# A relu layernorm times an 8192x8192 matrix on one core: x of the later row blocks loaded by GpSimd, behind its power, and not by SyncE

## The chip, the cores and the metric
One core of a Trainium2 chip runs the kernel; the chip's other cores do nothing. The metric is the device time of one execution in microseconds. The median of three runs before the change is 709.2 us (709.12 to 709.41). TensorE is called PE in the profile, VectorE DVE, ScalarE ACT, GpSimd POOL, SyncE SP; a q behind an engine's name means its sequencer, where transfers are issued.

## What is computed
```python
def _layernorm(x, axis=-1, eps=1e-05):
    m = jnp.mean(x, axis=axis, keepdims=True)
    v = jnp.var(x, axis=axis, keepdims=True)
    return (x - m) / jnp.sqrt(v + eps)

def reference(x, adj, L0_gnn_h):          # x, L0_gnn_h: 8192 x 128; adj: 8192 x 8192, all fp32
    h = jnp.maximum(_layernorm(x, axis=-1), 0.0)
    return x + 0.9 * (adj @ h) + 0.1 * L0_gnn_h
```
adj is the bulk: 256 MB of fp32, read once.

## The kernel before, in words
**Product.** The output is computed transposed, 128 features on the partitions, in 16 chunks (columns) of 512 rows of adj, with h as the stationary and adj (transposed on the host) as the moving operand. The contraction runs over 64 blocks of 128 rows of h. For precision both operands are split into a high part that TensorE takes at its fast rate (`fp32r`) and a low remainder: adj into `a_hi` (ScalarE, a copy, L305) and `a_lo` (VectorE, the subtraction, L349), h into `h_hi` (L282) and `h_lo` (L341). Each product is three matmuls: h_hi x a_hi, h_lo x a_hi, h_hi x a_lo (in the wide stage L451, L457, L462; in the tall stage L473, L474, L478). Only block 0 of h and the first six columns of adj for it are taken unsplit (L420).

**Pieces.** adj is read in 256 pieces of 128 x 2048 values, 1 MB each. The wide stage (pieces 0 to 127) does 8 chunks at once in the 8 banks of PSUM: two pieces per block of h, so block k is needed first at piece 2k. The tall stage (pieces 128 to 255) does one chunk after another with four blocks of h to a piece; by then all of h is there. A piece goes to one of 6 slots of `raw`, then to one of 3 slots of `a_hi` and `a_lo`. ScalarE and VectorE take the pieces in order; up to piece 39 VectorE makes `a_lo` in halves of 1024 columns (`LOW_PARTS`), up to piece 9 in quarters (`FINE_LOW`), then in one instruction. TensorE waits for each part of `a_lo` of a piece (`pe.wait_ge(lo_ready, ...)`) ahead of its L462.

**h.** The blocks of h are made in units: unit 0 is blocks 0 to 3, every later unit u = 1 to 30 two blocks, a = 2u + 2 and a + 1, needed by TensorE from piece due = 2a = 4u + 4 on. `GROUPS` is the same with block 0 by itself, so that group g = u + 1 is unit u. For a unit, VectorE takes statistics of x (`bn_stats`, L315, after waiting for `x_landed[u + 1]` in `wait_x`), aggregates them (L325) and adds epsilon (`var_eps`, L328); GpSimd takes the power -0.5 (`rstd`, L268); VectorE makes `shift` (L334); ScalarE makes h (`h_full`, L275) and h_hi; VectorE makes h_lo. x lies in a ring of 24 blocks.

**Order.** The order of each engine's work is written out by piece: tables say behind which piece's own work a step of h is done. For units with a < 20 (u = 1 to 8) the statistics come behind piece due - 6, the aggregate and the power behind due - 4, the shift behind due - 3; for the later ones the statistics come behind due - 6 and due - 5, the aggregate behind due - 5, the shift behind due - 4. h_full comes behind due - 2 and h_hi, h_lo behind due - 1.

**Queues.** SP issues nearly all transfers: for q = 0 to 255 `load_piece(q)`, which waits until the slot is free (from piece 8 on, until VectorE has made `a_lo` of piece q - 6), then at some q a load of residual data or a store. Ahead of `load_piece(q)` it issues the x of a unit where `LOAD_X_AT` says so (L217, in `load_x`): at q = due - 5 for a < 20, at due - 6 after. ScalarE issues x of blocks 1 to 3 and two halves of the first pieces at the start. GpSimd issues none; its loop is the 32 powers (L265 to L269).

Of the kernel before, what the change touches and what calls it, by code (L numbers as in the profile page):

```python
# [44 lines left out]
UNITS = [(0, FIRST)] + [(_b, _b + UNIT) for _b in range(FIRST, BLOCKS, UNIT)]  # L45
GROUPS = [(0, 1), (1, FIRST)] + UNITS[1:]
X_RING, H_RING = 24, 16
# [2 lines left out]

LATE = 20
LOAD_X_AT = {}
STATS_AT, AGGREGATE_AT, SHIFT_AT = {}, {}, {}
SCALE_AT, HIGH_H_AT = {}, {}
for _u in range(1, len(UNITS)):
    _a = UNITS[_u][0]
    _due = QUADS * _a
    if _a < LATE:  # L60
        LOAD_X_AT[_due - 5] = _u
        STATS_AT[_due - 6] = [_a, _a + 1]
        AGGREGATE_AT[_due - 4] = SHIFT_AT[_due - 3] = _u + 1
    else:
        LOAD_X_AT[_due - 6] = _u
        STATS_AT[_due - 6], STATS_AT[_due - 5] = [_a], [_a + 1]
        AGGREGATE_AT[_due - 5] = SHIFT_AT[_due - 4] = _u + 1
    SCALE_AT[_due - 2] = HIGH_H_AT[_due - 1] = _u
# [20 lines left out]
def parts(q):  # L89
    n = PARTS.get(q, 1)  # L90
    width = PIECE // n
    return [(i, slice(i * width, (i + 1) * width)) for i in range(n)]
# [19 lines left out]
def steps_through(q, halves, seg=QUAD - 1):  # L112

    own = next(i for i, end in enumerate(ends(q, halves)) if seg < end) + 1
    return sum(len(ends(k, halves)) for k in range(MIXED, q)) + own
# [6 lines left out]
def unit_of(k):  # L122
    return 0 if k < FIRST else 1 + (k - FIRST) // UNIT
# [9 lines left out]
def build(nc, x, adj_early, adj_wide, adj_tall, res, out):  # L133
# [4 lines left out]
    with ctx:  # L138
        def sb(name, shape, dt=fp32):
            return ctx.enter_context(nc.sbuf_tensor(name, shape, dt))  # L140

        def sem(name):
            return ctx.enter_context(nc.semaphore(name))
# [6 lines left out]
        x_sb = sb("x_sb", [P, X_RING, F])  # L150
# [13 lines left out]
        x_landed = [sem(f"x_landed{n}") for n in range(len(UNITS) + 1)]  # L164
# [13 lines left out]
        h_full_ready = sem("h_full_ready")  # L178
# [18 lines left out]
        def load_part(engine, q, i, cols):  # L197
            n = PARTS[q]
            at = (i % (n // 2)) * (PIECE // n)
            engine.dma_start(raw[:, q % RAW_SLOTS, cols],  # L200
                             adj_early[q, i // (n // 2), :, at:at + PIECE // n]
                             ).then_inc(part_landed[q % RAW_SLOTS][i], 16)

        def in_x(k):
            return k % X_RING
# [5 lines left out]

        @block.sync
        def _(sp):
            def load_x(n, a, b):
                if a >= X_RING:
                    sp.wait_ge(h_full_ready, unit_of(b - 1 - X_RING) + 1)
                sp.dma_start(x_sb[:, in_x(a):in_x(a) + b - a, :], x[:, a:b, :]).then_inc(x_landed[n], 16)  # L217

            def load_piece(q):
                if q >= RAW_SLOTS + NATIVE:  # L220
                    sp.wait_ge(lo_ready, steps_through(q - RAW_SLOTS, LOW_PARTS))
                elif q >= RAW_SLOTS:
                    sp.wait_ge(piece_used, q - RAW_SLOTS + 1)
                if q in PARTS:
                    for i, cols in parts(q):
                        if (q, i) not in BY_SCALAR:
                            load_part(sp, q, i, cols)
                else:
                    source = adj_wide[q - EARLY, :, :] if q < WIDE_PIECES else adj_tall[q - WIDE_PIECES, :, :]
                    sp.dma_start(raw[:, q % RAW_SLOTS, :], source).then_inc(raw_landed[q % RAW_SLOTS], 16)  # L230

            def load_residual(n):
                if n:
                    sp.wait_ge(residual_ready, n)
                sp.dma_start(res_sb[:, :, :], res[FINISH[n][0], :, :, :]).then_inc(res_landed, 16)

            def store(n):
                sp.wait_ge(finished_ready, n + 1)
                sp.dma_start(out[FINISH[n][0], :, :], finished[:, n % 2, :]).then_inc(stored[n % 2], 16)

            load_x(0, 0, 1)
            for q in range(PIECES):
                if q in LOAD_X_AT:
                    u = LOAD_X_AT[q]
                    load_x(u + 1, *UNITS[u])
                load_piece(q)
                if q in RES_LOAD_AT:
                    load_residual(RES_LOAD_AT[q])
                if q - RAW_SLOTS - 1 in FINISH_AT:
                    store(FINISH_AT[q - RAW_SLOTS - 1])  # L250
            last = len(FINISH) - 1
            sp.wait_ge(finished_ready, last + 1)
            sp.dma_start(out[FINISH[last][0], :, 0:SEG // 2],
                         finished[:, last % 2, 0:SEG // 2]).then_inc(stored[last % 2], 16)
            sp.wait_ge(finished_ready, last + 2)
            sp.dma_start(out[FINISH[last][0], :, SEG // 2:SEG],
                         finished[:, last % 2, SEG // 2:SEG]).then_inc(stored[last % 2], 16)
            sp.wait_ge(stored[(last + 1) % 2], 16 * ((last + 1) // 2))
            sp.wait_ge(stored[last % 2], 16 * (last // 2 + 2))

        @block.gpsimd
        def _(pool):
            nc.gpsimd.memset(warm[:, :], 0.0).then_inc(warm_ready, 1)
            nc.gpsimd.memset(exponent[:, :], -0.5).then_inc(exponent_ready, 1)
            pool.wait_ge(exponent_ready, 1)  # L265
            for g, (a, b) in enumerate(GROUPS):
                pool.wait_ge(var_eps_ready, g + 1)
                nc.gpsimd.tensor_tensor(rstd[:, a:b], var_eps[:, a:b], exponent[:, 0:b - a],  # L268
                                        ALU.pow).then_inc(rstd_ready, 1)  # L269

        @block.scalar
        def _(act):
# [40 lines left out]
        def _(dve):  # L313
# [30 lines left out]
            def low_a(q):  # L344
                for _, cols in steps(q, LOW_PARTS):
                    dve.wait_ge(hi_ready, steps_through(q, PARTS, cols.stop // SEG - 1))
                    if cols.start == 0 and q >= MIXED + SPLIT_SLOTS:
                        dve.wait_ge(piece_used, q - SPLIT_SLOTS + 1)
                    nc.vector.tensor_tensor(a_lo[:, q % SPLIT_SLOTS, cols], raw[:, q % RAW_SLOTS, cols],  # L349
                                            a_hi[:, q % SPLIT_SLOTS, cols].bitcast(fp32),  # L350
                                            ALU.subtract).then_inc(lo_ready, 1)
# [37 lines left out]
            for q in range(MIXED, PIECES):  # L389
                low_a(q)  # L390
                for k in STATS_AT.get(q, []):
                    wait_x(k)
                    last = statistics(k)
                    if any(k == end - 1 for _, end in GROUPS):
                        last.then_inc(stats_ready, 1)
                if q in AGGREGATE_AT:
                    aggregate(AGGREGATE_AT[q])
                if q in SHIFT_AT:
                    make_shift(SHIFT_AT[q])
                if q in HIGH_H_AT:  # L400
                    low_h(HIGH_H_AT[q])
                if q in FINISH_AT:
                    finish(FINISH_AT[q], slice(0, SEG))
                if q in RES_SUM_AT:
                    add_residual(RES_SUM_AT[q])
# [108 lines left out]
```

## Time and profile before

| | before |
|---|---|
| median of 3 runs | 709.2 us (709.12 to 709.41) |
| the profiled execution's own time | 709.23 us |
| its span in the profile | 707.4 us |
| PE, DVE, ACT, POOL busy | 702.4, 636.1, 531.6, 31.5 us |
| moved by the DMA engines | 285.75 MB, 404 GB/s in the mean |

The span runs from the first to the last recorded instruction; 1.8 us of the execution's time lie around it. Times of the rows below count from the start of the span. A row of the timeline gives start, duration, engine, line and operation, output<-inputs, how many instructions are merged in it, and in brackets how long the engine was idle before and what ended that.

### The profile page before, as it was taken

What the parts mean: (1) busy time and instruction counts of PE and PEld (TensorE: products, weight loads), DVE (VectorE), ACT (ScalarE), POOL (GpSimd) and SP (SyncE); (2) the same over time, 40 slices, a digit from 0 to 9 for tenths busy, and PEclk for the clock granted to TensorE, in tenths of its full rate; (3) what the DMA queues carried; (4) which work ended last, traced back from release to release, by engine and by line L of the source; (5) the groups of instructions that cost most, each with busy time, mean ns of one, the idle gap of its engine ahead of it and who ended that gap; (6) DMA issues with size and microseconds to landing.
All of it is one profiled execution on the core that took longest, in us unless ns stands there. A gap on an engine that the chain in (4) does not pass through costs nothing.

```text
span 707.4 us, 8192 instructions
## 1 busy us (share of the span) xinstructions
PE 702.4 (99%) x3088; PEld 578.4 (82%) x3088; DVE 636.1 (90%) x567; ACT 531.6 (75%) x465; POOL 31.5 (4%) x38
## 2 busy tenths in 40 slices
PE   8999999999999999999999999999999999999998
PEld 5888888888888888888888888888888888888886
DVE  5999999999989999999998888888988898889885
ACT  5899988788788788778776767676767676767673
POOL 1101110000000000000000000000000000000000
PEclk9999999999999999999999999999999999999999
DMA  9999999999999999999999999999999999999990
GB/s 365 417 418 420 416 419 416 419 416 418 420 416 419 417 419 417 419 416 420 421 418 418 388 409 389 404 401 399 414 421 414 424 420 423 422 419 422 406 414 21
DMA packets 46551, 285.75 MB, mean 404 GB/s; under 512 B 5168, under 2 KB 9520, under 8 KB 14000
## 3 DMA queue, kind: packets, MB, share of 16 engines
q1 hardware_dynamic: 46080, 283.99, 98.0%
q10 hardware_dynamic: 432, 1.25, 0.5%
q8 instruction: 24, 0.39, 0.2%
q14 instruction: 15, 0.12, 0.0%
HBM read 281.02 MB, written 4.19 MB: 403 GB/s over the span
## 4 chain that ended last, share of the span: by engine, by line
PE 99%; DMA 1%; DVE 0%; SPq 0%; DVEq 0%; issue 0%
PE acc L478 16%; PE acc L473 16%; PE acc L474 16%; PE acc L462 16%; PE acc L451 16%; PE acc L457 16%; PE acc L420 1%; DMA raw<-early_dram 1%; PE acc L433 0%; PE acc L437 0%; PE acc L429 0%; DVE finished L368 0%; SPq L217 0%; DVEq L138 0%; DVEq L367 0%
## 5 line engine op out<-in xcount | busy, mean ns | idle before, releaser
L349 DVE TENSOR_TENSOR a_lo<-raw,a_hi 128x2048 fp32r<-128x2048 f32 (+2 forms) x310 | 585.4, 1907 | 55.7 <-ACT a_hi L305 54.8
L305 ACT ACTIVATE a_hi<-raw 128x2048 fp32r<-128x2048 f32 (+1 forms) x370 | 498.9, 1378 | 159.8 <-PE acc L478 100.1
L473 PE MATMUL acc<-a_hi,h_hi 128*128 128x512 f32 x512 | 199.2, 389 | 0.0
L474 PE MATMUL acc<-a_hi,h_lo 128*128 128x512 f32 x512 | 199.2, 389 | 0.0
L451 PE MATMUL acc<-a_hi,h_hi 128*128 128x512 f32 x504 | 167.5, 389 | 0.0
L457 PE MATMUL acc<-a_hi,h_lo 128*128 128x512 f32 x504 | 167.5, 389 | 0.0
L478 PE MATMUL acc<-a_lo,h_hi 128*128 128x512 f32 x512 | 136.8, 389 | 0.0
L462 PE MATMUL acc<-a_lo,h_hi 128*128 128x512 f32 x504 | 134.7, 389 | 0.0
L473 PEld LDWEIGHTS acc<-a_hi,h_hi 128*128 128x128 f32 x512 | 96.1, 188 | 20.0
L478 PEld LDWEIGHTS acc<-a_lo,h_hi 128*128 128x128 f32 x512 | 96.1, 188 | 20.0
L474 PEld LDWEIGHTS acc<-a_hi,h_lo 128*128 128x128 f32 x512 | 96.1, 188 | 19.9
L457 PEld LDWEIGHTS acc<-a_hi,h_lo 128*128 128x128 f32 x504 | 94.6, 188 | 19.7
L451 PEld LDWEIGHTS acc<-a_hi,h_hi 128*128 128x128 f32 x504 | 94.6, 188 | 19.7
L462 PEld LDWEIGHTS acc<-a_lo,h_hi 128*128 128x128 f32 x504 | 94.5, 188 | 19.8 <-DVE a_lo L349 0.2
L268 POOL TENSOR_TENSOR rstd<-var_eps,exponent 128x2 f32<-128x2 f32 (+2 forms) x32 | 30.9, 967 | 301.3 <-DVE var_eps L328 301.3
L275 ACT ACTIVATE h_full<-x_sb,shift,rstd 128x128 f32<-128x128 f32 x63 | 27.2, 479 | 4.5 <-DVE shift L334 4.5
L315 DVE BATCH_NORM_STATS2 stats<-x_sb 128x6 f32<-128x128 f32 x64 | 17.4, 285 | 3.8 <-DMA x_sb<-x_dram 3.8
L341 DVE TENSOR_TENSOR h_lo<-h_full,h_hi 128x256 fp32r<-128x256 f32 (+1 forms) x31 | 13.2, 427 | 2.1 <-ACT h_hi L282 2.1
L368 DVE SCALAR_TENSOR_TENSOR finished<-acc,residual 128x512 f32<-128x512 f32 (+1 forms) x17 | 11.0, 653 | 3.9 <-PE acc L478 3.9
L282 ACT ACTIVATE h_hi<-h_full 128x256 fp32r<-128x256 f32 (+1 forms) x31 | 12.6, 407 | 0.1
L357 DVE SCALAR_TENSOR_TENSOR residual<-res_sb 128x512 f32<-128x512 f32 x16 | 10.9, 684 | 0.0
L325 DVE BATCH_NORM_AGGREGATE mean_var<-stats 128x2 f32<-128x6 f32 x64 | 7.9, 165 | 0.8
(21 smaller groups left out, 31.5 us busy)
## 6 DMA issues: line engine op xcount, KB each, us to landing
raw<-tall_dram SPq DMA_DIRECT2D x128, 1024.0 KB, 8.3
raw<-wide_dram SPq DMA_DIRECT2D x126, 1024.0 KB, 11.8
res_sb<-res_dram SPq DMA_DIRECT2D x16, 512.0 KB, 10.2
x_sb<-x_dram SPq DMA_DIRECT2D x30, 128.0 KB, 11.9
out_dram<-finished SPq DMA_DIRECT2D x15, 256.0 KB, 8.6
raw<-early_dram ACTq DMA_DIRECT2D x2, 512.0 KB, 6.6
raw<-early_dram SPq DMA_DIRECT2D x2, 512.0 KB, 6.2
out_dram<-finished SPq DMA_DIRECT2D x2, 128.0 KB, 1.8
```

Of the source, the lines that this page charges most:

```text
L268: nc.gpsimd.tensor_tensor(rstd[:, a:b], var_eps[:, a:b], exponent[:, 0:b - a], ALU.pow).then_inc(rstd_ready, 1)
L275: last = nc.scalar.activation(h_full[:, in_h(k), :], x_sb[:, in_x(k), :], ACT.Relu, bias=shift[:, k:k + 1], scale=rstd[:, k:k + 1])
L305: nc.scalar.activation(a_hi[:, q % SPLIT_SLOTS, cols], raw[:, q % RAW_SLOTS, cols], ACT.Copy).then_inc(hi_ready, 1)
L315: return nc.vector.bn_stats(stats[:, k, :], x_sb[:, in_x(k), :])
L341: nc.vector.tensor_tensor(h_lo[:, a:b, :], h_full[:, in_h(a):in_h(a) + b - a, :], h_hi[:, a:b, :].bitcast(fp32), ALU.subtract).then_inc(h_ ...
L349: nc.vector.tensor_tensor(a_lo[:, q % SPLIT_SLOTS, cols], raw[:, q % RAW_SLOTS, cols], a_hi[:, q % SPLIT_SLOTS, cols].bitcast(fp32), ALU.s ...
L451: nc.tensor.matmul(acc[:, quad * QUAD + j, :], h_hi[:, k, :], a_hi[:, slot, cols], start=False, stop=False)
L457: nc.tensor.matmul(acc[:, quad * QUAD + j, :], h_lo[:, k, :], a_hi[:, slot, cols], start=False, stop=False)
L462: last = nc.tensor.matmul(acc[:, quad * QUAD + j, :], h_hi[:, k, :], a_lo[:, slot, cols], start=False, stop=(k == BLOCKS - 1))
L473: nc.tensor.matmul(bank, h_hi[:, k, :], a_hi[:, slot, cols], start=(k == 0), stop=False)
L474: nc.tensor.matmul(bank, h_lo[:, k, :], a_hi[:, slot, cols], start=False, stop=False)
L478: last = nc.tensor.matmul(bank, h_hi[:, k, :], a_lo[:, slot, cols], start=False, stop=(k == BLOCKS - 1))
```

## The change
x of units 1 to 30 is no longer issued by SP but by GpSimd: in the loop over groups, after the power of group g (which is unit g - 1), GpSimd issues x of unit g. The wait for a free place in the ring, from block 24 on, goes with it. SP keeps x of block 0, the pieces, the residual data and the stores. Statistics, aggregates and all else keep their places. The first of the moved loads, x of unit 1, now stands behind the power for blocks 1 to 3.

```diff
@@ -50,19 +50,17 @@
 LATE = 20
-LOAD_X_AT = {}
 STATS_AT, AGGREGATE_AT, SHIFT_AT = {}, {}, {}
 SCALE_AT, HIGH_H_AT = {}, {}
 for _u in range(1, len(UNITS)):
     _a = UNITS[_u][0]
     _due = QUADS * _a
     if _a < LATE:
-        LOAD_X_AT[_due - 5] = _u
         STATS_AT[_due - 6] = [_a, _a + 1]
         AGGREGATE_AT[_due - 4] = SHIFT_AT[_due - 3] = _u + 1
     else:
-        LOAD_X_AT[_due - 6] = _u
         STATS_AT[_due - 6], STATS_AT[_due - 5] = [_a], [_a + 1]
         AGGREGATE_AT[_due - 5] = SHIFT_AT[_due - 4] = _u + 1
     SCALE_AT[_due - 2] = HIGH_H_AT[_due - 1] = _u
@@ -211,11 +209,6 @@
         @block.sync
         def _(sp):
-            def load_x(n, a, b):
-                if a >= X_RING:
-                    sp.wait_ge(h_full_ready, unit_of(b - 1 - X_RING) + 1)
-                sp.dma_start(x_sb[:, in_x(a):in_x(a) + b - a, :], x[:, a:b, :]).then_inc(x_landed[n], 16)
-
@@ -238,11 +231,8 @@
-            load_x(0, 0, 1)
+            sp.dma_start(x_sb[:, 0:1, :], x[:, 0:1, :]).then_inc(x_landed[0], 16)
             for q in range(PIECES):
-                if q in LOAD_X_AT:
-                    u = LOAD_X_AT[q]
-                    load_x(u + 1, *UNITS[u])
                 load_piece(q)
@@ -260,6 +250,12 @@
         @block.gpsimd
         def _(pool):
+            def load_x(u):
+                a, b = UNITS[u]
+                if a >= X_RING:
+                    pool.wait_ge(h_full_ready, unit_of(b - 1 - X_RING) + 1)
+                pool.dma_start(x_sb[:, in_x(a):in_x(a) + b - a, :], x[:, a:b, :]).then_inc(x_landed[u + 1], 16)
+
@@ -267,6 +263,8 @@
                 pool.wait_ge(var_eps_ready, g + 1)
                 nc.gpsimd.tensor_tensor(rstd[:, a:b], var_eps[:, a:b], exponent[:, 0:b - a],
                                         ALU.pow).then_inc(rstd_ready, 1)
+                if 0 < g < len(UNITS):
+                    load_x(g)
```

## Rows read from the trace of the kernel before
**Rows 1.** The page: busy shares, clock and GB/s in 40 slices, the chain by engine.
```profile
PE 702.4 (99%) x3088; PEld 578.4 (82%) x3088; DVE 636.1 (90%) x567; ACT 531.6 (75%) x465; POOL 31.5 (4%) x38
...
PEclk9999999999999999999999999999999999999999
...
GB/s 365 417 418 420 416 419 416 419 416 418 420 416 419 417 419 417 419 416 420 421 418 418 388 409 389 404 401 399 414 421 414 424 420 423 422 419 422 406 414 21
...
PE 99%; DMA 1%; DVE 0%; SPq 0%; DVEq 0%; issue 0%
```
**Rows 2.** Waits: engine, line <- whom: us in total, times, longest us.
```profile
ACT a_hi L305 <- DMA raw<-wide_dram: 44.0, 72, 1.9
...
DVE stats L315 <- DMA x_sb<-x_dram: 3.8, 1, 3.8
...
PEld acc L462 <- DVE a_lo L349: 0.2, 1, 0.2
```
**Rows 3.** Timeline of PE: first matmuls on data, then sets of L462.
```profile
6.48 5.39 PE L420 MATMUL acc<-raw,h_full 128*128 128x512 f32 x12 [0.79 <-DMA raw<-early_dram]
...
28.54 1.07 PE L462 MATMUL acc<-a_lo,h_hi 128*128 128x512 f32 x4
...
39.41 1.10 PE L462 MATMUL acc<-a_lo,h_hi 128*128 128x512 f32 x4
...
50.35 0.62 PE L462 MATMUL acc<-a_lo,h_hi 128*128 128x512 f32 x2
...
91.15 0.39 PE L462 MATMUL acc<-a_lo,h_hi 128*128 128x512 f32 x1
```
**Rows 4.** Windows of VectorE: stretch, its length, DVE busy (instructions), clock, DMA share, GB/s.
```profile
25.51:36.78 11.27, 10.77 (x22) 1.00 1.01 415
...
57.58:67.90 10.32, 10.29 (x16) 1.00 1.02 419
```
**Rows 5.** Timeline of VectorE.
```profile
14.68 0.48 DVE L315 BATCH_NORM_STATS2 stats<-x_sb 128x6 f32<-128x128 f32 x2
...
25.51 0.48 DVE L315 BATCH_NORM_STATS2 stats<-x_sb 128x6 f32<-128x128 f32 x2
25.91 2.48 DVE L349 TENSOR_TENSOR a_lo<-raw,a_hi 128x512 fp32r<-128x512 f32 x4
...
36.78 0.48 DVE L315 BATCH_NORM_STATS2 stats<-x_sb 128x6 f32<-128x128 f32 x2
...
42.60 2.36 DVE L349 TENSOR_TENSOR a_lo<-raw,a_hi 128x1024 fp32r<-128x1024 f32 x2
...
47.22 0.48 DVE L315 BATCH_NORM_STATS2 stats<-x_sb 128x6 f32<-128x128 f32 x2
47.71 2.37 DVE L349 TENSOR_TENSOR a_lo<-raw,a_hi 128x1024 fp32r<-128x1024 f32 x2
...
99.07 0.28 DVE L315 BATCH_NORM_STATS2 stats<-x_sb 128x6 f32<-128x128 f32 x1
...
109.82 0.29 DVE L315 BATCH_NORM_STATS2 stats<-x_sb 128x6 f32<-128x128 f32 x1
```
**Rows 6.** Transfers of x: issues, KB each, median us from issue to landing.
```profile
x_sb<-x_dram SPq DMA_DIRECT2D x30, 128.0 KB, 11.9
...
x_sb<-x_dram SPq DMA_DIRECT2D x1, 64.0 KB, 3.0
```
**Rows 7.** Timeline of GpSimd: its powers.
```profile
6.78 0.86 POOL L268 TENSOR_TENSOR rstd<-var_eps,exponent 128x3 f32<-128x3 f32 x1 [1.62 <-DVE var_eps L328]
20.78 1.08 POOL L268 TENSOR_TENSOR rstd<-var_eps,exponent 128x2 f32<-128x2 f32 x1 [13.14 <-DVE var_eps L328]
31.57 1.15 POOL L268 TENSOR_TENSOR rstd<-var_eps,exponent 128x2 f32<-128x2 f32 x1 [9.71 <-DVE var_eps L328]
42.77 1.61 POOL L268 TENSOR_TENSOR rstd<-var_eps,exponent 128x2 f32<-128x2 f32 x1 [10.05 <-DVE var_eps L328]
...
94.41 1.61 POOL L268 TENSOR_TENSOR rstd<-var_eps,exponent 128x2 f32<-128x2 f32 x1 [8.72 <-DVE var_eps L328]
102.77 0.81 POOL L268 TENSOR_TENSOR rstd<-var_eps,exponent 128x2 f32<-128x2 f32 x1 [6.75 <-DVE var_eps L328]
```

## The prediction
> **What bounds the kernel now.** I read the page's busy shares and its chain first [rows 1]. TensorE is busy 702.4 of 707.4 us, the chain that ended last is 99% TensorE, and its clock is at the full level in all 40 slices: nothing that only frees another engine or a queue can be worth much. The first matmul on data starts at 6.48 us, after 0.79 us of wait for the first piece of adj [rows 3], which is issued ahead of every transfer that the change touches. So the question is not what TensorE gains, but who could make it wait. The waits [rows 2] say that nobody does: its longest on a split piece of adj is 0.2 us, once. But the transfers are busy: ScalarE waited 44.0 us for pieces [rows 2], and the queues moved 416 to 420 GB/s in most slices of the first half [rows 1].
>
> VectorE is the engine with the least room. One piece costs TensorE 2.72 us (from 50.35 to 91.15 us are 15 pieces, [rows 3]), four of them, one unit of h, 10.88 us. VectorE is busy 10.29 us of the 10.32 from the statistics of unit 5 to those of unit 6 [rows 4]: it gains 10.88 - 10.31 = 0.57 us on TensorE per unit (10.31 with the gaps between instructions). Its lead is short. After the statistics of unit 2 it ends piece 7 at 25.91 + 2.48 = 28.39 us [rows 5], and TensorE takes the last part of that piece at 28.54 + 3 x 0.227 = 29.22 [rows 3] (0.227 us is 2.72 / 12 matmuls): a lead of 0.83 us. After those of unit 3 it is gone: the set of four at 39.41 lasts 1.10 us where the others last 1.07 [rows 3], and that is where the 0.2 us wait of [rows 2] falls; after unit 4, piece 15 ends at 47.71 + 2.37 = 50.08 [rows 5] and its second half is needed at 50.35 + 0.45 = 50.80 [rows 3], a lead of 0.72 us; from there it grows by 0.57 us a unit, to about 3.0 at unit 8.
>
> **Removed from SP.** 30 issues [rows 6]. SP itself is on no chain, so its time is worth nothing. The same bytes are still moved; pieces 3 to 5 find the queue shorter by 128 KB, 0.31 us at 419 GB/s, which at best adds 0.3 us to VectorE's early lead. The waits of ScalarE that this might shorten end in no wait of TensorE. Gain: 0.
>
> **Moved.** On SP, x of a unit was issued five or six pieces ahead in a list that itself runs six pieces ahead of the compute, and took 11.9 us to land (median, [rows 6]), behind four pieces of its own queue; bn_stats never waited for it after block 0. Now the issue stands behind GpSimd's power of the unit before. What is left from the end of that power [rows 7] to the bn_stats that needs x [rows 5]:
> - unit 1: 6.78 + 0.86 = 7.64, needed at 14.68: 7.0 us
> - unit 2: 20.78 + 1.08 = 21.86, needed at 25.51: 3.65 us
> - unit 3: 32.72, needed at 36.78: 4.06 us, of which 11.27 - 10.77 = 0.50 us is idle time of VectorE [rows 4] that falls away once it is late: 3.56
> - unit 4: 44.38, needed at 47.22: 2.84 us; units 5 to 8 repeat this to 0.01 us
> - unit 9: 96.02, needed at 99.07: 3.05 us
> - unit 10: 103.58, needed at 109.82: 6.24 us, since from here the schedule leaves three pieces between the power and the next statistics, not two; units 11 to 30 are alike.
>
> So eight units, 2 to 9, have some 3 us each. **How long does x take?** The trace has no transfer issued by GpSimd, so I bound it. The shortest row is x of block 0, 64 KB on an otherwise idle chip: 3.0 us from issue to landing [rows 6]. Faster than that it will not be: this load is twice as large (64 KB more at 419 GB/s is 0.16 us) and the DMA engines are busy: 3.2 us. The upper end is 11.9 us, were it to stand behind the pieces as before. In between, on a queue of its own it should take turns with the pieces. x has 128 rows of 1 KB, 8 for each of 16 DMA engines; a piece has rows of 8 KB, and one of those takes 8192 B / (419 / 16 GB/s) = 0.31 us. With a turn for every row x takes 3.2 + 8 x 0.31 = 5.7 us, with four rows to a turn 3.2 + 2 x 0.31 = 3.8 us. I take the middle, 4.8 us, from the end of the power to landing; it is nearer to the row of 3.0 than to that of 11.9, because the backlog ahead of x is what the move takes away.
>
> **The price at 4.8 us.** bn_stats waits on VectorE; behind it, in order, stands the low part of the next piece, for which TensorE waits, and later h_lo. Nothing passes it.
> - unit 2: late 4.8 - 3.65 = 1.15, less the lead of 0.83: TensorE loses 0.32
> - unit 3: late 1.24; before it VectorE is busy 10.77 us, a gain of only 10.88 - 10.77 = 0.11: loses 1.13
> - units 4 to 8: late 1.96, less the 0.57 regained: 1.39 each, 6.95
> - unit 9: late 1.75 - 0.57 = 1.18
> - units 1 and 10 to 30: 0; x lands within their 6.2 to 7.0 us. Above 6.2 us that cover is gone, and 21 units would be late too.
>
> Sum 9.6 us. TensorE has no idle time later in which to make it good. Slots of raw are freed later by as much, but then the queue holds its pieces ready, which adds nothing. For GpSimd the issue costs nothing: its next power comes about 10 us later [rows 7], and the wait for a free place in the ring, before units 11 and up, is for an h made long before. Against the profiled execution's own 709.23 us this gives 718.8; the median of the runs is 0.03 less, so 718.8 stands. Around this point each microsecond of landing time is worth 8 us of kernel time, one for each late unit.
>
> **The rivals.**
> 1. **In time.** x lands within 3.5 us. Then units 2 and 3 are not late, units 4 to 8 are 0.66 us late against 0.57 regained and a lead of 0.72, and TensorE loses nothing: 709.2, no change. For it: 3.0 us in [rows 6]. Against it: that was an idle chip and an issue from SP. The point from which it decides is a landing in 3.5 us. 13%.
> 2. **Few turns.** Rows travel four to a turn and x lands after 3.8 us. Unit 2 takes 0.15 of the lead and unit 3 0.24 - 0.11 = 0.13, which leaves 0.55; units 4 to 8 lose 0.96 - 0.57 = 0.39 each, unit 9 0.18: 2.13 - 0.55 = 1.6 us, 710.8. The Trainium skill (DMA: Bandwidth & Descriptors, SWDGE vs HWDGE vs iDMA) has a DMA engine change queues only at the border of a packet, which is preferably up to 4096 B; four rows of 1 KB would be one, and the sum by it is this rival's. No row here shows it. 20%.
> 3. **Held by VectorE.** The power that starts at 42.77 [rows 7] ends at 44.38, 0.60 us after the end of the half of a_lo that VectorE began at 42.60 (42.60 + 2.36 / 2 = 43.78, [rows 5]), though 0.81 us is enough for it at 102.77 [rows 7]: GpSimd is held until VectorE's instruction ends. If making the issue is held like that too, by one more half of 1.2 us, x takes 6.0 us: 9.6 + 8 x 1.2 = 19.2, 728.4; if it is held more than once, the later units are late too and it goes to 738 or so. The Trainium skill (SBUF — State Buffer, Who interferes with whom) speaks against it: a VectorE operation with two SBUF inputs contends only with GpSimd instructions that read SBUF, and making descriptors writes. 19%.
> 4. **No overtaking.** x waits behind the pieces as now, 11.9 us. Late by 9.06 less 0.57 in units 4 to 8, 42 us, by about as much in the three others, 24 us, and by 5.7 us less what is regained in each of 21 more, about 105: 880. Against it: the queues are different. 3%.
> 5. **Freed stream.** Pieces come sooner and the kernel is faster. It could give back the 0.2 us wait at L462 and little more, since the rest of TensorE's 5.0 us idle lies before 6.48 us and behind the last matmul: 709.0. A larger gain needs a cause that the trace does not show. 3%.
>
> **The numbers.** The forecast (landing in 4.3 to 6 us) has 42%, 718.8 us. A difference under 0.2%, 1.4 us, can't be told from none. Slower by more: the forecast, rivals 3 and 4 and most of rival 2, 79%; within: rival 1 and the rest of 2, 18%; faster 3%. The range takes in rival 1, since it is too likely to be left out, and ends inside rival 3: 709.0 to 730.0, which is any landing up to 6.2 us; what is left out is rival 4, rival 5 and half of 3.
>
> **What would show it.** In the profile after: bn_stats waits for x_sb in eight units between 25 and 110 us, 1 to 2 us each, 14 us in all, and in none after; the matmuls of a_lo wait for VectorE about 1.4 us per unit there; the issues on GpSimd land in 4.3 to 6 us; the powers keep their times. From 120 us on the two traces run in parallel, shifted by 9 to 10 us. I am wrong if bn_stats doesn't wait (rival 1), if units 10 and up wait as well (rivals 3, 4), if the first load of the new queue takes so long that unit 1 waits, or if VectorE's own instructions get longer beside the issues.

## The result and the profile after

The changed kernel takes 718.78 us in the median of four runs (718.16 to 720.36), the kernel before 709.26 beside it; the ratio is 1.0138, 95% interval [1.0125, 1.015]. The prediction said 718.8 us, 709.0 to 730.0, slower with 79%. Its profiled execution is the longest of the four, 720.36 us with a span of 718.5; 11.1 us more than before.

The page of the changed kernel (busy shares, clock, GB/s in 40 slices, chain by engine), which answers to [rows 1]:

```profile
PE 707.2 (98%) x3088; PEld 578.9 (81%) x3088; DVE 636.1 (89%) x567; ACT 532.2 (74%) x465; POOL 48.2 (7%) x68
...
GB/s 367 418 420 353 411 327 385 417 418 417 418 417 418 417 419 419 417 419 417 405 407 391 403 396 390 397 394 400 414 421 421 422 421 422 421 421 423 406 417 22
...
PE 85%; DMA 7%; DVE 6%; POOL 1%; issue 1%; SPq 0%; ACT 0%; DVEq 0%
```

VectorE is exactly as busy as before; what is new is a chain that leaves TensorE. The slices with 353, 327 and 385 GB/s lie between 54 and 126 us; after that the two profiles are alike. The waits say who waited, answering to [rows 2]:

```profile
DVE stats L313 <- DMA x_sb<-x_dram: 17.9, 9, 3.8
ACT h_full L273 <- DVE shift L332: 16.7, 8, 4.3
PEld acc L460 <- DVE a_lo L347: 11.4, 14, 2.1
PE acc L460 <- DVE a_lo L347: 5.7, 7, 1.7
...
ACT a_hi L303 <- DMA raw<-wide_dram: 3.9, 8, 1.0
```

bn_stats waits nine times; one is block 0's old wait. The other eight stand in VectorE's timeline (L313; the bracket is the wait):

```profile
28.29 0.49 DVE L313 BATCH_NORM_STATS2 stats<-x_sb 128x6 f32<-128x128 f32 x2 [3.10 <-DMA x_sb<-x_dram]
...
41.04 0.49 DVE L313 BATCH_NORM_STATS2 stats<-x_sb 128x6 f32<-128x128 f32 x2 [2.01 <-DMA x_sb<-x_dram]
...
53.89 0.49 DVE L313 BATCH_NORM_STATS2 stats<-x_sb 128x6 f32<-128x128 f32 x2 [2.53 <-DMA x_sb<-x_dram]
...
65.60 0.48 DVE L313 BATCH_NORM_STATS2 stats<-x_sb 128x6 f32<-128x128 f32 x2 [1.38 <-DMA x_sb<-x_dram]
...
76.12 0.49 DVE L313 BATCH_NORM_STATS2 stats<-x_sb 128x6 f32<-128x128 f32 x2 [0.20 <-DMA x_sb<-x_dram]
...
86.80 0.49 DVE L313 BATCH_NORM_STATS2 stats<-x_sb 128x6 f32<-128x128 f32 x2 [0.35 <-DMA x_sb<-x_dram]
...
100.91 0.49 DVE L313 BATCH_NORM_STATS2 stats<-x_sb 128x6 f32<-128x128 f32 x2 [3.79 <-DMA x_sb<-x_dram]
...
112.24 0.29 DVE L313 BATCH_NORM_STATS2 stats<-x_sb 128x6 f32<-128x128 f32 x1 [1.01 <-DMA x_sb<-x_dram]
```

These are units 2 to 9 and no others, 14.4 us together (the prediction: 13.9). GpSimd's timeline has the new issues (L257) behind the powers, answering to [rows 7]:

```profile
20.39 1.09 POOL L264 TENSOR_TENSOR rstd<-var_eps,exponent 128x2 f32<-128x2 f32 x1 [12.27 <-DVE var_eps L326]
21.45 0.58 POOL L257 DMA_DIRECT2D x_sb<-x_dram  x1
...
72.99 0.58 POOL L257 DMA_DIRECT2D x_sb<-x_dram  x1
...
94.19 0.58 POOL L257 DMA_DIRECT2D x_sb<-x_dram  x1
```

and the landing times of x, asked of the trace issue by issue, are 6.8, 5.6, 5.4, 4.3, 3.1, 3.3, 6.7 and 3.9 us for units 2 to 9, 3.7 us for unit 10 and 5.5 to 6.5 us for all later ones. Two of these answers, for the issues at 72.99 and 94.19, and the page's line over all:

```profile
x_sb<-x_dram POOLq DMA_DIRECT2D x1, 128.0 KB, 3.1
...
x_sb<-x_dram POOLq DMA_DIRECT2D x1, 128.0 KB, 6.7
...
x_sb<-x_dram POOLq DMA_DIRECT2D x30, 128.0 KB, 5.7
```

Not one value, then, but at least two, and what goes with them is how many pieces stand in SP's queue. The two pieces issued last before x took 9.7 us to land before unit 3, 7.1 before unit 4, 5.5 before unit 5 and 4.8 before unit 6 (medians). Counted in bytes (what SP had issued less what its queue had moved), 3.8, 2.4 and 1.3 MB were outstanding when x of units 2, 3 and 4 was issued, 1.0 MB for units 5 to 10, and 1.9 to 2.4 MB for every later one. A late VectorE frees the slots of raw later, so SP issues its pieces later, and the queue stays short up to unit 10. The DMA engines are not free in the meantime: while x of unit 6 landed in 3.1 us they moved 425 GB/s; it is over whole stretches of 20 us that they fall to 400 GB/s and less, 327 in the one with unit 8's wait behind it.

Unit 8 fits neither value. The queue was as short as for units 6 and 7, and 45 of the 48 packets of its x had started 2.9 us after the issue, as there; the last three came 3.8 to 6.4 us after it. Something held up one or a few of the DMA engines, and no run shows what; the same x landed after 5.1 us in the run with only units 2 to 9 and after 4.5 us in that with rows of 4 KB. The windows of the changed kernel in stretches of 20 us (stretch, length, DVE busy, clock, DMA share, GB/s):

```profile
40.00:60.00 20.00, 16.36 (x26) 1.00 0.97 389
60.00:80.00 20.00, 18.39 (x26) 1.00 0.97 386
80.00:100.00 20.00, 16.70 (x25) 1.00 1.02 400
100.00:120.00 20.00, 17.98 (x28) 0.91 0.86 327
```

The window of unit 6's landing, with the busy time of PE, PEld, DVE, ACT and POOL, and the packets of x in the 2.94 us from unit 8's issue (packets, MB, share):

```profile
72.99:76.09 3.10, 3.10 (x16) 2.55 (x15) 2.94 (x4) 2.40 (x6) 0.58 (x2) 1.00 1.02 425
```

```profile
q0 software_dynamic: 45, 0.12, 11.2%
```

### The profile page after: what moved, and what is told of

Read it like the earlier page. It is cut to its first block, busy times and chain, and to the rows that moved or that the text cites. A ratio compares the mean times of both kernels' runs of the same rounds, so it can differ in the third digit from the quotient of the medians.

```text
span 718.5 us, 8192 instructions
## 1 busy us (share of the span) xinstructions
PE 707.2 (98%) x3088; PEld 578.9 (81%) x3088; DVE 636.1 (89%) x567; ACT 532.2 (74%) x465; POOL 48.2 (7%) x68
## 3 DMA queue, kind: packets, MB, share of 16 engines
q0 software_dynamic: 1440, 3.93, 1.4%
## 4 chain that ended last, share of the span: by engine, by line
PE 85%; DMA 7%; DVE 6%; POOL 1%; issue 1%; SPq 0%; ACT 0%; DVEq 0%
PE acc L476 16%; PE acc L472 16%; PE acc L471 16%; PE acc L460 12%; PE acc L449 12%; PE acc L455 12%; DMA x_sb<-x_dram 5%; DVE a_lo L347 5%; DMA raw<-wide_dram 2%; POOL rstd L264 1%; DVE h_lo L339 0%; DVE stats L313 0%; DVE var_eps L326 0%; DVE mean_var L323 0%; SPq L198 0%
## 5 line engine op out<-in xcount | busy, mean ns | idle before, releaser
L460 PE MATMUL acc<-a_lo,h_hi 128*128 128x512 f32 x504 | 137.4, 392 | 6.5 <-DVE a_lo L347 5.7
L460 PEld LDWEIGHTS acc<-a_lo,h_hi 128*128 128x128 f32 x504 | 94.1, 188 | 30.3 <-DVE a_lo L347 11.4
L313 DVE BATCH_NORM_STATS2 stats<-x_sb 128x6 f32<-128x128 f32 x64 | 17.4, 285 | 17.9 <-DMA x_sb<-x_dram 17.9
L257 POOL DMA_DIRECT2D x_sb<-x_dram x30 | 17.6, 586 | 0.0
```

The source lines that it names most:

```text
L257: pool.dma_start(x_sb[:, in_x(a):in_x(a) + b - a, :], x[:, a:b, :]).then_inc(x_landed[u + 1], 16)
L313: return nc.vector.bn_stats(stats[:, k, :], x_sb[:, in_x(k), :])
L460: last = nc.tensor.matmul(acc[:, quad * QUAD + j, :], h_hi[:, k, :], a_lo[:, slot, cols], start=False, stop=(k == BLOCKS - 1))
```

## The experiments

The last column has the median landing of the run's late-issued x, or a range where it varied. Theory: nothing costs but a landing after bn_stats' turn on VectorE, in units 2 to 9, and it costs what VectorE's lead does not cover. Rivals: the issues from GpSimd cost by themselves; only the moment matters and not the queue; and for the landing itself, turns by packet against a fixed latency. Edits are against the changed kernel unless the text says before.

| run | us, median | ratio to before, 95% | x lands, us |
|---|---|---|---|
| one power earlier | 709.52 | 0.9996 to 1.0013 | 5.6 |
| only units 2 to 9 | 719.11 | 1.0127 to 1.0157 | 6.9 to 3.1 |
| only units 10 to 30 | 709.63 | 0.9996 to 1.0014 | 5.7 |
| statistics later | 711.87 | 1.0023 to 1.005 | 5.6 |
| SP, same moment | 721.72 | 1.0141 to 1.021 | 12.7, then 4.8 to 7.2 |
| pieces in two transfers | 731.72 | 1.029 to 1.0347 | 5.4 |
| ScalarE's queue | 710.54 | 1.0009 to 1.0027 | 7.0 |
| rows of 4 KB | 719.76 | 1.0138 to 1.0169 | 5.3 |
| x of two units at once | 710.05, one run | | 6.5 |
| ScalarE's queue, rows of 4 KB | 717.38, one run | | 5.9 |
| unit 3 alone | 712.13 | 1.0029 to 1.0051 | 6.6 |
| unit 8 alone | 709.27 | 0.9995 to 1.0012 | 5.8 |

**One power earlier.** The same 30 issues on the same queue.

```diff
-                if 0 < g < len(UNITS):
-                    load_x(g)
+                if g + 1 < len(UNITS):
+                    load_x(g + 1)
```

> x of a unit still comes on GpSimd's queue, but one power earlier: x of unit g + 1 behind the power of group g, x of unit 1 behind the very first power. The window from the power to bn_stats grows by a unit, to 13 us and more. Theory (lateness: only a landing after bn_stats' turn costs, in units 2 to 9): no wait of bn_stats after block 0, and 709.2 us, within 0.5. Rival (issue cost: transfers issued by GpSimd hold up VectorE or the DMA engines wherever they stand): 30 issues are still there, so most of the 9.5 us stays, 715 to 719 us.

709.52 us, not to be told from before. Of the waits of bn_stats only block 0's is left:

```profile
DVE stats L313 <- DMA x_sb<-x_dram: 3.2, 1, 3.2
```

The issues cost nothing by themselves: the first rival is out.

**Only units 2 to 9, and only 10 to 30**, on GpSimd's queue; the rest stays on SP, in the kernel before.

```diff
-                if q in LOAD_X_AT:
+                if q in LOAD_X_AT and not (2 <= LOAD_X_AT[q] <= 9):
...
+                if 2 <= g <= 9 and g < len(UNITS):
+                    load_x(g)
```

> Only x of units 2 to 9 comes on GpSimd's queue behind the power of the unit ahead; units 1 and 10 to 30 come from SP as before. Lateness theory: the whole loss is in these eight, 718 to 720 us, with 13 to 16 us of waits of bn_stats. Issue-cost rival: 8 of 30 issues, so 8/30 of 9.5 us: about 711.8 us.

> Only x of units 10 to 30 comes on GpSimd's queue behind the power of the unit ahead; units 1 to 9 come from SP as before. Lateness theory: it lands after 5.5 to 6.5 us as in the changed kernel, just inside the window of 6.2 to 6.8 us, and VectorE's lead of 3 us covers the rest: 709.2 us, within 0.5. Issue-cost rival: 21 of 30 issues, about 715.9 us.

719.11 and 709.63 us: the eight units carry the whole loss, and the other 21 nothing. In the first, bn_stats waited 12.5 us in those eight (3.18, 2.68, 1.65, 1.53, 0.17, 0.45, 2.23 and 0.56), with landings from 6.9 down to 3.1 us: the same running down of the queue.

**Statistics later**, by one piece of a_lo, in units 2 to 8.

```diff
-        STATS_AT[_due - 6] = [_a, _a + 1]
+        STATS_AT[_due - 6 if _u == 1 else _due - 5] = [_a, _a + 1]
```

> The changed kernel with the statistics of units 2 to 8 one piece of a_lo later (behind piece due - 5, just ahead of their aggregate). Their window grows from 2.84 to about 5.4 us (unit 2: 6.3, unit 3: 6.2), unit 9 keeps its 3.05. Lateness theory: x landed after 5.4 to 6.8 us in the changed kernel wherever the queue of pieces was full, so each unit is 0 to 1.3 us late against 0.57 regained, and unit 9 eats into the lead only: 709.2 to 712 us. Issue-cost rival: nothing changes, 718 to 719 us.

711.87 us, at the upper end. Units 2 to 8 wait 0.20 to 0.72 us each; unit 9, which was left as it is, waits 2.64:

```profile
104.20 0.30 DVE L313 BATCH_NORM_STATS2 stats<-x_sb 128x6 f32<-128x128 f32 x1 [2.64 <-DMA x_sb<-x_dram]
```

With no long waits 2.0 MB or more of pieces are outstanding at each issue, and x of units 2 to 9 lands after 5.5 to 7.0 us. A wider window takes most of the loss away, as lateness wants it.

**SP, same moment.** The kernel before, x of units 2 to 8 issued late by SP.

```diff
-        LOAD_X_AT[_due - 5] = _u
+        LOAD_X_AT[_due - 5 if _u == 1 else _due - 1] = _u
```

> The kernel before, with x of units 2 to 8 issued by SP, but only ahead of piece due - 1, which is about when the changed kernel's power of the unit ahead is done (SP reaches that place once a_lo of piece due - 8 is made). Same moment, other queue. If the queue matters because x overtakes the pieces on GpSimd's: x of unit 2 lands after about 12 us, bn_stats waits 8 us and more for it, and since the queue drains in each wait, 2 to 6 us for each of the others: 730 to 755 us. If only the moment matters (no overtaking): about the changed kernel's time, 716 to 720 us.

721.72 us (719.67 and 723.77), between the two expectations. x of unit 2 landed after 12.7 us and bn_stats waited 7.90 for it, as the first theory said:

```profile
33.36 0.48 DVE L315 BATCH_NORM_STATS2 stats<-x_sb 128x6 f32<-128x128 f32 x2 [7.90 <-DMA x_sb<-x_dram]
...
55.29 0.49 DVE L315 BATCH_NORM_STATS2 stats<-x_sb 128x6 f32<-128x128 f32 x2 [0.72 <-DMA x_sb<-x_dram]
```

But that one wait let the queue run down: x of units 3 and 4 landed after 4.8 and 5.3 us, unit 3 did not wait at all, and the others waited up to 2.62. The backlog that x would stand behind is fed by the engine that waits for x, so it can't hold it up for long. Overtaking matters for the first late unit; I had priced it as if the backlog stayed. Nor is all of the loss the wait's: behind it TensorE's clock was granted at its lower level (the window of 31.60 to 38.60; stretch, length, busy time and count of PE, PEld, DVE, ACT, POOL, then clock, DMA share, GB/s):

```profile
31.60:38.60 7.00, 4.11 (x9) 2.72 (x10) 5.24 (x11) 2.48 (x6) 0.00 (x0) 0.51 0.86 318
```

7.0 us at 0.51 are about 3.4 us of full clock, and both executions have the same mean clock, 0.995. That leaves about 9 us for seven late units on SP's queue, no more than eight cost on GpSimd's.

**Pieces in two transfers, rows of 4 KB.** What sets the 5.6 us?

```diff
+                    for c in (slice(0, PART), slice(PART, PIECE)):
+                        sp.dma_start(raw[:, q % RAW_SLOTS, c], source[:, c]).then_inc(raw_landed[q % RAW_SLOTS], 16)
```

(the waits for a piece go to 32), and, in the second run, one transfer again (the host lays adj out to match):

```diff
+                    sp.dma_start(raw[:, q % RAW_SLOTS, :].rearrange("p (i c) -> p i c", i=2),
+                                 source.rearrange("i p c -> p i c")).then_inc(raw_landed[q % RAW_SLOTS], 16)
```

> The changed kernel with every piece of adj from the third on moved by two transfers of 512 KB (1024 columns each, rows of 4 KB) and not by one of 1 MB (rows of 8 KB). With the queue of pieces full, x of units 10 to 30 landed after 5.5 to 6.5 us in the changed kernel, some 2.4 us over the 3.1 us of an empty queue. If each of x's packets waits for a fixed number of rows of a piece, or for the rest of one transfer of a piece: that 2.4 us halves, x lands after 4.3 to 4.6 us, and the kernel comes down to 711 to 715 us. If the 2.4 us is the latency of busy memory whatever the rows: 5.5 us and 717 to 720 us.

> The changed kernel with every piece of adj from the third on still moved by one transfer of 1 MB, but with rows of 4 KB, twice as many. Beside the run with two transfers of 512 KB this tells row from transfer: if x's packets wait for rows, x lands after 4.3 to 4.6 us here too, if they wait for what is left of one transfer, after 5.6 us as in the changed kernel, with its 717 to 720 us.

x lands after 5.4 and 5.3 us, where the changed kernel has 5.6 to 5.7. That is near the fixed latency of the first expectation (5.5) and far from the 4.3 to 4.6 of the turns. So the 2.4 us are neither the rest of a transfer (the two runs agree) nor all rows; only 0.3 us follows the row. The times tell little of x, since rows of 4 KB are moved at 404 to 410 GB/s (slices of the first half) where rows of 8 KB got 416 to 420, and now TensorE's stages are short of pieces too: 26.8 us (two transfers) and 20.6 us (one) of ScalarE's waits for pieces of the tall stage, none before. The first is a further 12 us longer (11.4 between the profiled executions), and its trace says by what: bn_stats waits 20.3 us in units 2 to 9 where the second waits 12.0, since x of units 6 to 9 lands after 5.0 to 6.3 us and not after 3.2 to 4.5, and it has two stretches at the lower clock, 3.41 us each at 0.50 (from 32.98 and from 84.18), 3.4 us of full clock, where the second has none before the end. With two transfers x's first packet starts 2.7 to 3.7 us after the issue and not 2.2 to 2.3, with the same 1.0 MB outstanding, which are two transfers instead of one; why that matters is open.

**ScalarE's queue.** x issued by ScalarE.

```diff
+                if q + 1 in SCALE_AT and SCALE_AT[q + 1] + 1 < len(UNITS):
+                    load_x(SCALE_AT[q + 1] + 1)
```

> The changed kernel with x of units 1 to 30 issued by ScalarE, on its own queue, about 1 us before the power of the unit ahead ends (behind a_hi of piece due - 7, x of unit 1 ahead of h of blocks 1 to 3). If taking turns with the pieces makes the landing, packet by packet, x is 8 packets of 1 KB per DMA engine here and 2 of 4 KB on GpSimd's queue: with a turn for each packet it lands later than 5.6 us, 7 us or more, and bn_stats waits longer: 720 us and more. If a queue of its own gives x the same wait whoever issues it: it lands after 5 to 5.6 us, less GpSimd's own time to make it, and with the earlier issue the kernel comes to 711 to 716 us.

The landing is 7.0 us, as the turns by packet had it, and yet the time is 710.54 us, below both numbers: x was issued at 19.05 us for unit 2, not at 21.45, which more than makes up for it in most units: bn_stats waited in three of the eight, 1.34 us at most, and in five later ones (units 10, 13, 18, 26 and 29), 1.69 us at most, where VectorE has a lead. I had put that head start at 1 us; it is 2.4.

Packets of x: the page's queue rows give 1440 for 30 transfers on GpSimd's queue, 3 for each of 16 DMA engines (2 of 4 KB and one that signals), and on ScalarE's (4752 - 432) / 30 = 144, 9 for each (8 of one row and one that signals). The queue's row (packets, MB, share) of the changed kernel:

```profile
q0 software_dynamic: 1440, 3.93, 1.4%
```

and that of ScalarE's queue in the run with it:

```profile
q10 hardware_dynamic: 4752, 5.18, 2.1%
```

That gives a form: landing = c + packets x time of one row of a piece (0.31 us at 8 KB, 0.16 at 4 KB). GpSimd's queue: 5.6 - 2 x 0.31 = 5.0 and 5.3 - 2 x 0.16 = 5.0. ScalarE's: 7.0 - 8 x 0.31 = 4.5. Two more runs put it to the test, **x of two units in one transfer** (on the first run's kernel: a, b span two units, behind every second power) and **ScalarE's queue with rows of 4 KB**:

> As the first run (x one power early on GpSimd's queue, queue of pieces always full, x landed after 5.6 us there), but x of two units in one transfer behind every second power: 256 KB, per DMA engine 4 packets of 4 KB and not 2. With one turn of 0.31 us (a row of a piece) for each packet and 128 KB more of its own: 5.6 + 2 x 0.31 + 0.31 = 6.5 us. Were the landing a fixed latency of the busy engines, only its own bytes come on top: 5.9 us. The kernel's time stays at 709.2 to 710 us.

> The run with x on ScalarE's queue (8 packets of 1 KB per DMA engine, landed after 7.0 us) together with that of pieces in rows of 4 KB. With a turn of one row for each packet of x, 8 turns get 0.16 us shorter each: 5.8 us, where two turns on GpSimd's queue saved 0.3 us (5.6 to 5.3). Were it a fixed saving from shorter rows, 6.7 us here too.

The issues of x with their KB and median landing, of the first and of the second:

```profile
x_sb<-x_dram POOLq DMA_DIRECT2D x15, 256.0 KB, 6.5
```

```profile
x_sb<-x_dram ACTq DMA_DIRECT2D x30, 128.0 KB, 5.9
```

6.5 us expected and measured; 5.8 expected, 5.9 measured, each from one execution with 15 and 30 such transfers. Each packet of x waits one row of the other queue's. What stays open is c: 4.5 us (4.6 from the last run) and 5.0 us with about 2 MB or more outstanding on SP's queue, where the whole landing is 3.1 us with 1 MB. The packets say where most of the difference lies: the first one of x starts nearly always 3.7 to 3.9 us after the issue on GpSimd's queue in the one case and 2.0 to 2.3 us in the other. In the changed kernel, 2.06 us from the issue for unit 6 (72.99) and 3.74 us from that for unit 11 (126.71) have packets of SP's queue alone, at its full share of the DMA engines both times (the only rows of those two stretches: packets, MB, share):

```profile
q1 hardware_dynamic: 111, 0.91, 104.5%
```

```profile
q1 hardware_dynamic: 286, 1.56, 101.1%
```

It is not GpSimd's own work on the transfer: on ScalarE's queue the first packet starts 3.4 to 3.5 us after the issue. So 1.7 of the 1.9 us pass before x's first packet moves, and no run here shows why.

**One unit alone**, in the kernel before.

```diff
-                if q in LOAD_X_AT:
+                if q in LOAD_X_AT and not (LOAD_X_AT[q] == 3):
...
+                if g == 3 and g < len(UNITS):
+                    load_x(g)
```

> The kernel before with x of unit 3 alone on GpSimd's queue behind the power of unit 2. The queue of pieces is full, so it lands after 5.6 us and more; the window is 3.56 us and VectorE's lead there about 0.1: TensorE loses 1.9 us, 711.1 us. With the prediction's 4.8 us of landing it would be 710.3 us; if stalls of VectorE are made good later, 709.2.

> The kernel before with x of unit 8 alone on GpSimd's queue behind the power of unit 7. It lands after 5.6 us against a window of 2.83: bn_stats waits 2.8 us, as long as in the bad units of the changed kernel, but VectorE's lead is 2.96 us there: TensorE loses nothing, 709.2 to 709.6 us. If the wait counted in full: 712.0.

Unit 3: bn_stats waits 2.71 us and TensorE loses 2.71 us, its matmuls of a_lo (L470) 8.15 us apart over two pieces, 36.85 to 45.00, where two pieces take 5.44. Unit 8: bn_stats waits 2.88 us and TensorE loses nothing; 712.13 against 709.27 us. The timeline of TensorE in the run with unit 3:

```profile
36.85 1.07 PE L470 MATMUL acc<-a_lo,h_hi 128*128 128x512 f32 x4
41.46 0.73 PE L470 MATMUL acc<-a_lo,h_hi 128*128 128x512 f32 x2 [1.73 <-DVE a_lo L357]
42.60 0.73 PE L470 MATMUL acc<-a_lo,h_hi 128*128 128x512 f32 x2 [0.40 <-DVE a_lo L357]
45.00 1.07 PE L470 MATMUL acc<-a_lo,h_hi 128*128 128x512 f32 x4
```

and that of VectorE in the run with unit 8:

```profile
91.60 0.48 DVE L323 BATCH_NORM_STATS2 stats<-x_sb 128x6 f32<-128x128 f32 x2 [2.88 <-DMA x_sb<-x_dram]
```

The same wait costs everything where the lead is 0 and nothing where it is 3 us. Unit 3 alone is 1.0 us above what I expected, because x took 6.6 us there and not 5.6; its six runs spread from 710.38 to 713.55.

None of the twelve beats the kernel before.

## Why the prediction was right, and where it was not

**The bound, the lead and the windows held.** The waits came in units 2 to 9 and nowhere else. The windows from the power's end to bn_stats' turn, in the changed kernel: unit 2 21.48 to 25.19, 3.71 us (3.65 forecast); unit 3 3.58 (3.56); unit 4 2.90 (2.84); unit 8 2.90. The lead's arithmetic is shown by the two runs with one unit each.

**The landing of 4.8 us was right only as a mean.** The eight are 39.1 us together, 4.9 each. As the prediction put it, 3.2 us plus the middle of two and eight turns, each part is off: the turns are two (rival 2 had that right, 3.8 us), and the base is 5.0 us under load, not 3.2; the row of 3.0 us from a queue that was still empty is no lower half for one that is full. With 5.6 us in all eight units the sum would have been 9.6 + 8 x 0.8 = 16 us, 725. What brought it back is what I had not thought of: the waits shorten SP's queue, and x then lands in 3.1 to 4.3 us. The prediction had the slots of raw freed later too, but said that the queue "holds its pieces ready"; it did not. Two errors of opposite sign cancel, and of the eight landings only three (5.6, 5.4 and 4.3 us) lie in the 4.3 to 6 us on which the forecast stood; 718.8 against 718.78 owes much to luck. The arithmetic behind the landing held: the measured waits less the prediction's own leads and gains give 2.3, 1.9, 2.0, 0.8, 0, 0, 2.6 and 0.4 us for units 2 to 9, 10.0 together, where TensorE lost 9.4 (the 11.1 of the span less 1.7 for its clock, see below).

**The price by unit** was even in the forecast and is not so in the trace. What TensorE lost, from the starts of L460 two pieces apart less 5.44 us: unit 2 2.4 us (0.3 forecast), 3 1.9 (1.1), 4 2.0 (1.4), 5 0.9 (1.4), 6 and 7 0 (1.4 each), 8 4.2 (1.4; 1.7 of the 4.2 are the clock's), 9 0 (1.2). That is 11.3 us before rounding; the first matmul came 0.2 us earlier (6.27 for 6.48 us), which leaves the 11.1 us of the span. Unit 8 is the largest of them by the straggling packets above, so its share is chance as well.

**Rival 1** (in time) asked for 3.5 us, which x met only behind waits that had already been paid. **Rival 3** (held by VectorE) is out: the 30 issues take 0.58 us each (the first 0.72) beside back-to-back halves of a_lo, while the powers go on taking 1.61 us there. The rule of the Trainium skill (SBUF — State Buffer, Who interferes with whom) agrees with these two rows. **Rival 4** had the right first wait (7.9 us on SP's queue) and a price that was wrong by far: 66 us over units 2 to 9, where the run on SP lost 12.5 in units 2 to 8, some 3.4 of them by the clock, because the backlog was taken as standing. Whether its 105 us for the later units would shrink in the same way was not tried. **Rival 5**: the issues that SP no longer makes gained nothing, 709.52 us with x one power earlier.

**The cover of units 10 to 30 is thin.** x lands after 5.5 to 6.5 us in a window of 6.24: it held, and a VectorE lead of some 3 us stands behind it.

## What to carry to other kernels

A transfer moved behind a later event must be priced by its landing under the load that it will meet; the landing beside an empty queue is a bound and not a half of the answer. Count how far ahead of its reader it is issued, subtract, and let the reader's lead over the bounding engine absorb what it can: 2.9 us late was free at one place and 2.7 us late cost 2.7 at another. And where the reader that waits is also the one that frees the slots of the busy queue, its waits shorten that queue (from 3.8 to 1.0 MB here), so that the price of the first late transfer can't be multiplied by their number.

## What had not been expected of the hardware

**TensorE's clock fell in the profiled execution.** The page's tenths show 9 in every slice, but behind unit 8's wait the matmuls stretch. TensorE's timeline of the changed kernel:

```profile
102.57 0.73 PE L460 MATMUL acc<-a_lo,h_hi 128*128 128x512 f32 x2 [1.65 <-DVE a_lo L347]
103.71 0.84 PE L460 MATMUL acc<-a_lo,h_hi 128*128 128x512 f32 x2 [0.40 <-DVE a_lo L347]
104.35 0.63 PE L449 MATMUL acc<-a_hi,h_hi 128*128 128x512 f32 x1
```

and the window that follows (stretch, length, busy time and count of PE, PEld, DVE, ACT, POOL, then clock, DMA share, GB/s):

```profile
103.70:108.00 4.30, 4.29 (x12) 3.39 (x13) 4.26 (x8) 2.19 (x4) 1.29 (x1) 0.60 0.76 265
```

After this wait the granted clock is 0.60 in the mean from 103.7 to 108.0 us, the lower level, 1.2 GHz, for the most part, and the chain has matmuls at 0.43 us where they are 0.23 apart: the step of 9.65 us from 98.04 to 107.69 is 4.2 us over two pieces, though bn_stats waited 3.79 and there was a lead to use up. 4.30 us at 0.60 are 1.7 us of full clock, so 1.7 us of the 11.1 are the clock's. The execution's mean clock is 0.998; the three others have 0.999 to 1.000 and end at 718.16 to 718.88 us, 1.7 us earlier in the median. It does not follow every such wait: behind units 2, 3 and 4 of the same trace (TensorE idle for 0.92 to 0.99 us) the clock stayed at 1.00, and so it did with only units 2 to 9 late (idle for up to 1.6 us). When it falls, a wait of VectorE costs TensorE more than its length.

**A packet of x waits for one row of the other queue**, and c is 5.0 us from GpSimd and 4.5 from ScalarE with about 2 MB or more outstanding on SP's queue. For 128 KB in rows of 1 KB the queue from GpSimd is the faster by 1.4 us (5.6 against 7.0), since it joins four rows to a packet. The Trainium skill (DMA: Bandwidth & Descriptors, SWDGE vs HWDGE vs iDMA) gives packets of preferably up to 4096 B for the software queue, and the counts agree (2 packets of 4 KB for the 8 rows of 1 KB that each DMA engine moves).
